# Graph attention layer of a four-layer network: odd units with exponentials taken straight from the sum, and the maximum with one on VectorE

## The reference

```
h = jnp.maximum(_layernorm(x, axis=-1), 0.0)
...
x = h @ weight
el = x @ a_l
er = x @ a_r
mask = adj != 0
scores = el[:, None] + er[None, :]
attn = jnp.exp(jax.nn.leaky_relu(scores, negative_slope=0.2))
attn = jnp.where(mask, attn, 0.0)
denom = jnp.maximum(attn.sum(axis=-1, keepdims=True), 1e-12)
A = attn / denom
out = A @ x + b
```

## Time and profile before

| | us |
|---|---|
| median of 3 runs | 2030.96 (2030.25 to 2031.25) |
| the profiled execution | 2032.97 |
| its span in the trace | 2031.2 |
| attention layer, first y to last y | 597.2 to 868.0 |

### The profile page before, as it was taken

One profiled execution on the slowest core, in us unless ns is written; L12 is line 12 of the kernel. 1 busy time (PEld: TensorE's weight loads), 2 busy tenths in 40 slices (PEclk: granted clock), 3 DMA queues, 4 the chain that ended last, 5 costly groups with the idle time before them and its releaser, 6 DMA issues.

```text
span 2031.2 us, 24901 instructions
## 1 busy us (share of the span) xinstructions
PE 1867.2 (92%) x9423; PEld 1309.6 (64%) x9423; DVE 1505.4 (74%) x2278; ACT 1366.1 (67%) x1760; POOL 13.4 (1%) x15
## 2 busy tenths in 40 slices
PE   4877889699988999999999989899999999999998
PEld 4877888488878989955555556544555555554554
DVE  6222226888877888887878753499898898988986
ACT  4222221466668999988777630399898898988984
POOL 0000000000010000000000000000000000000000
PEclk9999999899999999989999999999999999999999
DMA  9999997688866767669999789533343333334230
GB/s 382 424 424 424 424 425 279 238 323 314 318 250 221 270 243 265 249 219 361 354 327 363 265 311 373 178 119 114 114 154 116 114 119 117 132 123 146 99 99 21
DMA packets 88794, 498.12 MB, mean 245 GB/s; under 512 B 9265, under 2 KB 13362, under 8 KB 39266
## 3 DMA queue, kind: packets, MB, share of 16 engines
q1 hardware_dynamic: 84354, 494.34, 65.1%
q10 hardware_dynamic: 4320, 2.20, 0.4%
HBM read 456.55 MB, written 39.94 MB: 244 GB/s over the span
## 4 chain that ended last, share of the span: by engine, by line
PE 52%; DMA 15%; ACT 14%; DVE 14%; issue 5%; SPq 0%; ACTq 0%; DVEq 0%
PE bank L1972 15%; DMA work<-in_adj_rows 12%; PE bank L1946 4%; ACT work L755 4%; PE bank L1785 3%; ACT work L750 3%; PE bank L1787 3%; PE bank L1786 3%; PE bank L1858 2%; DVE work L1581 2%; PE bank L1980 2%; PE bank L1981 2%; ACT work L906 2%; PE bank L1979 2%; PE bank L1863 2%
## 5 line engine op out<-in xcount | busy, mean ns | idle before, releaser
L1972 PE MATMUL bank<-work,reg 128*128 128x512 f32 x760 | 359.2, 597 | 14.6 <-DVE ring L1532 7.9
L906 ACT ACTIVATE work<-x,e 128x512 f32<-128x512 f32 x552 | 355.1, 709 | 0.4 <-ACT linebuf L871 0.4
L1581 DVE TENSOR_TENSOR work<-work,ring 128x1536 f32<-128x1536 f32 x184 | 321.2, 1749 | 9.2 <-ACT work L906 9.0
L1696 PE MATMUL bank<-reg,ring 128*128 128x128 f32 x2048 | 251.0, 284 | 52.3 <-DMA ring<-in_adj_units 29.7
L1696 PEld LDWEIGHTS bank<-reg,ring 128*128 128x128 f32 x2048 | 243.4, 199 | 58.8 <-issue 37.7
L1816 PE MATMUL bank<-reg,ring 128*128 128x129 f32 x2048 | 242.8, 281 | 26.0 <-DVE ring L1275 25.7
L1816 PEld LDWEIGHTS bank<-reg,ring 128*128 128x128 f32 x2048 | 238.2, 197 | 29.9 <-DVE ring L1275 19.1
L1972 PEld LDWEIGHTS bank<-work,reg 128*128 128x128 f32 x760 | 142.6, 190 | 136.2 <-issue 112.0
L1979 PE MATMUL bank<-s_lo,h_hi 128*128 128x512 f32 x240 | 186.0, 775 | 4.9 <-DVE a_lo L1560 3.7
L1275 DVE SCALAR_TENSOR_TENSOR ring<-ring,work 128x2048 f32<-128x2048 f32 x64 | 147.2, 2300 | 39.3 <-ACT work L755 39.2
L1170 DVE TENSOR_TENSOR a_lo<-ring,a_hi 128x2048 fp32r<-128x2048 f32 x64 | 147.5, 2315 | 17.9 <-ACT a_hi L706 17.5
(11 more groups left out here) (295 smaller groups left out, 3073.7 us busy)
## 6 DMA issues: line engine op xcount, KB each, us to landing
ring<-in_adj_units SPq DMA_DIRECT2D x320, 1024.0 KB, 5.5
work<-in_adj_rows SPq DMA_DIRECT2D x38, 1024.0 KB, 22.6
ring<-masks SPq DMA_DIRECT2D x64, 512.0 KB, 5.7
ring<-in_adj_rows SPq DMA_DIRECT2D x26, 1024.0 KB, 22.4
masks<-work SPq DMA_DIRECT2D x48, 512.0 KB, 8.7
masks<-ring SPq DMA_DIRECT2D x16, 512.0 KB, 8.2
x<-lines SPq DMA_DIRECT2D x8, 768.0 KB, 10.4
ring<-lines SPq DMA_DIRECT2D x8, 768.0 KB, 7.9
```

What stands on the lines that cost most here:

```text
L906: last = act.activation(tiles(n)[:, k * W:(k + 1) * W], guard(c, k), ACT.Sigmoid, bias=e6[:, t * SCORES + k:t * SCORES + k + 1], scale=-1.0)
L1581: dve.tensor_tensor(tv, tv, spread(ring[:, ring_at("out", g, q * W, W)], HEADS, 1), ALU.mult).then_inc(s_y, 1)
L1696: last = pe.matmul(o, ring[:, first:first + P], reg1[:, t * P:(t + 1) * P], start=t == 0 and i == 0, stop=t == T - 1 and i == Q - 1)
L1972: return pe.matmul(bank[1 + k][:, :], reg1[:, t * P:(t + 1) * P], tiles(c * T + t)[:, k * W:(k + 1) * W], start=t == 0, stop=t == T - 1)
```

## The change

Every second unit (n odd, `straight(n)`) is made in another way. ACT takes all its four quarters as Exp straight from `reg4` with the bias `er08`, with no rectifier, and there is no exponential of the whole unit and no quarter on DVE. DVE then takes the maximum with 1 over the whole unit in place (128 x 2048), counts it on a new semaphore `s_gone`, waits for it, and does y(n). Even units stay as they were. The counts of `s_gmax` and `s_grelu` now go by even units.

```
-        def by_dve(n):
-
-            return 2 if n % 2 else 1
+        def straight(n):
+
+            return n % 2 == 1
...
+        s_gone = sem("gat_at_least_one")
...
-                    for q in range(by_dve(n), Q):
+                    for q in range(0 if straight(n) else 1, Q):
                         m = g * Q + q
-                        last = act.activation(gunit(n)[:, q * W:(q + 1) * W], reg4[:, at(c, W, 0, W)], ACT.Relu,
-                                              bias=er08[:, m:m + 1])
-                    last.then_inc(s_grelu, 1)
-                    act.wait_ge(s_gmax, n + 1)
-                    act.wait_ge(s_grelu, n + 1)
-                    act.activation(gunit(n), gunit(n), ACT.Exp).then_inc(s_gexp, 1)
+                        last = act.activation(gunit(n)[:, q * W:(q + 1) * W], reg4[:, at(c, W, 0, W)],
+                                              ACT.Exp if straight(n) else ACT.Relu, bias=er08[:, m:m + 1])
+                    if straight(n):
+                        last.then_inc(s_gexp, 1)
+                    else:
+                        last.then_inc(s_grelu, 1)
+                        act.wait_ge(s_gmax, n // 2 + 1)
+                        act.wait_ge(s_grelu, n // 2 + 1)
+                        act.activation(gunit(n), gunit(n), ACT.Exp).then_inc(s_gexp, 1)
...
-                for q in range(by_dve(n)):
-                    m = g * Q + q
-                    last = dve.tensor_scalar(gunit(n)[:, q * W:(q + 1) * W], reg4[:, at(c, W, 0, W)],
-                                             er08[:, m:m + 1], 0.0, ALU.add, ALU.max)
-                last.then_inc(s_gmax, 1)
+                dve.tensor_scalar(gunit(n)[:, 0:W], reg4[:, at(c, W, 0, W)], er08[:, g * Q:g * Q + 1], 0.0,
+                                  ALU.add, ALU.max).then_inc(s_gmax, 1)
...
-                    if n + 1 < C * G:
+                    if n + 1 < C * G and not straight(n + 1):
                         gat_max(n + 1)
...
                     dve.wait_ge(s_gexp, n + 1)
+                    if straight(n):
+                        dve.tensor_scalar(gunit(n), gunit(n), 1.0, None, ALU.max).then_inc(s_gone, 1)
+                        dve.wait_ge(s_gone, n // 2 + 1)
                     y = ring[:, ring_at("gat", g)]
                     dve.scalar_tensor_tensor(y, y, 0.0, gunit(n), ALU.not_equal, ALU.mult).then_inc(s_gy, 1)
```

## The result

The changed kernel takes 2029.57 us (median of 20 runs, 2027.31 to 2032.22), the kernel before 2031.7 us (20 runs, 2028.32 to 2037.65). The medians are 2.1 us apart. The ratio over all runs is 0.9985, 95% interval 0.9979 to 0.9991 (the quotient of the medians alone is 0.9989): faster by 0.15%, 3 us, and less than the 0.2% that the prediction set as the bound for faster. The profiled execution took 2029.65 us, with a span of 2027.9 (forecast 2029.9; before 2032.97, with 2031.2).

A forecast was written before the change was run, and what follows sets the result against it. One chain bounds each chunk: DVE's node results, a quarter, ACT's exponential and `root`, unit 5, ACT's remaining units. Terms -1.1 - 1.8 - 0.35 + 0.15 = -3.1 us take the median from 2030.96 to 2027.9; range 2021.5 to 2034.5.

The forecast's parts named there:

- wide maximum: DVE's in-place maximum over 2048 numbers in each odd unit, taken at 1.22 us, plus 0.03 for its semaphore wait.
- node results start: On DVE, node results start 2.21 us after y(1) instead of 3.00, as the quarters for unit 3 are gone.
- first quarter of unit 5: ACT starts unit 5's four quarters at 14.54 us, 5.33 after the exponential of unit 4 starts.
- y(5): On DVE, y(5) at 18.44 us instead of 18.75; of 0.79 us won, 0.48 have gone.
- first chunk, change at y(9): First chunk, order set by the layer before: -1.1 us, between -0.4 and -2.
- second chunk: Chunk without `gat_project` and `store_hT`: y(9) at 31.13 us against 32.94 measured before, -1.8 us.
- third to seventh chunk together: Five steady chunks, each 33.35 us instead of 33.42: -0.35 us.
- last chunk to its last y: Last chunk, which ends with y(7): +0.15 us.
- the walk: One attention-layer chunk retraced from y(1) with measured distances: 33.35 us instead of 33.42, DVE setting the pace after y(5).
- Rival 1: DVE's maximum costs more, up to 2.29 us each, 3.2 us per chunk more, total up to 2052 us; chance 0.12.
- Rival 2: DVE's 2.0 us wait for unit 5 vanishes, seven chunks each gain 2.0, total 2014 us; chance 0.07.
- Rival 3: PE becomes the bound through low-clock spells, 34.1 us per chunk with two in each, total about 2033 us; chance 0.09.

The follow-up runs named there:

- `root` early: Changed kernel with root (logarithm and exponential of the norm) moved on ACT between unit 4's quarters and its exponential; 2015.15 us, ratio to before 0.9916.
- units 1, 3, 5 and `root` early: Changed kernel with unit 7 made as before and root moved on ACT between unit 4's quarters and its exponential; 2013.76 us, ratio to before 0.9902.

## Why the prediction was right

The mechanism held, and so did its times. From the start of the node results to the next y(1) they count from y(1) at 0 in the chunk from 702.64:

| step | forecast | measured |
|---|---|---|
| wide maximum | 1.22 | 1.220 (median of 32) |
| node results start | 2.21 | 2.21 |
| y(2) | 6.48 | 6.49 |
| ACT starts exponential of unit 4 | 9.21 | 9.21 |
| first quarter of unit 5 | 14.54 | 14.54 |
| y(5) | 18.44 | 18.46 |
| y(6) | 21.68 | 21.69 |
| y(7) | 27.28 | 27.28 |
| next y(1) | 33.35 | 33.34 |
| first chunk, change at y(9) | -1.1 | -0.9 |
| second chunk | -1.8 | -1.7 |
| third to seventh chunk together | -0.35 | -0.4 |
| last chunk to its last y | +0.15 | +0.15 |

- The sum of -3.1 us came out as -2.9 at the last y (865.73 to 862.82); the span fell by 3.3, of which 0.4 us arose behind the layer. That the total agrees this well is in part luck. The 0.02 us of the walk hold for the steady chunks, but the layer's first y alone lies anywhere from 595.5 to 597.7 us in the seven profiles with unit 1 straight, and single runs of the kernel before spread over 9 us.
- One reading was loose: "three engines within 10% of the period" is true of ACT and PE, while DVE, at 29.09 of 33.42 us, is 13% below. Nothing in the walk uses it.
- The seven quarters from 717.18 (four Exp, three Relu) end after 4.38 us: six distances of 0.61 and one duration of 0.71, the same as for Relu alone. Exp costs ACT the same as Relu at this size.
- The weighed price of the maximum went to the row: 1.22 us, not the 1.13 us estimated from the cycles in "VectorE: DVE Perf Modes" of the Trainium skill.
- In the first chunk the maximum of unit 5 took 2.06 us beside POOL, as the quarter in the earlier trace rows had let one fear; it is one of 32.
- Rival 1 (a dear maximum) did not come, but its slope did: 3.79 us per chunk for 1.25 us on each of the four, three of them in the chain. Rival 2 (DVE's wait goes) did not come by itself, and came with `root` early: 2.05 us per chunk, against 2.0 in the rival. Rival 3 (PE's clock falls more often) did not come; the clock fell less often, see below.

One thing was less good: that one reordering would bring what the change did not was in the text only as the condition of rival 2, called out of reach because of the order, though the order is a line of the kernel.

## What to carry to other kernels

When an instruction is taken from a busy engine, look first at which of its instances stands ahead of the chain's hand-over: here one of four carried the gain (0.79 us per chunk), and the others gave nearly all of it back with what they added behind it (unit 7 0.46 us, units 1 and 5 together 0.25). Where three engines are within some 13% of the period, walk one period with the measured distances before and after; counting ACT's work said that 3.1 us per chunk were to be had, the walk said 0.07, and the chunks gave 0.1. And where an engine waits in front of work on which a slow, independent step (here two table loads) follows, move that step into the wait.

## What was not expected

- PE's clock. Before, PE waited 1.6 to 2.5 us for y(2) in seven chunks, and behind three of these waits (2.51, 2.16 and 2.15 us) the granted clock was 0.50, as at 748.38; behind another of 2.16 it was 1.00. With the change the same wait is 0.4 to 1.2 us, and in no chunk behind the first did the clock fall:

```profile
711.48 11.27 PE L1820 MATMUL bank<-reg,ring 128*128 128x129 f32 x96 [1.12 <-DVE ring L1279]
...
732.26 10.99 PE L1820 MATMUL bank<-reg,ring 128*128 128x129 f32 x96 [1.41 <-DVE ring L1279]
```

  The rival had asked whether more waits might lower the clock: two waits of 1.1 to 1.4 us in a chunk left it at 2.4 GHz, and next to waits of 2.15 or 2.16 us before it was at 1.2 GHz in two cases of three. With the maximum taken twice PE waits 2.66 to 2.67 us once in each of the third to seventh chunks, and the granted clock is 0.50 next to each of the five. By "TensorE: Matmul & The Clock Gate" of the Trainium skill, Part 1, low is the clock's state at rest and work releases it; the trace agrees in so far as the clock stayed up where the waits were short. The low spells cost nothing before either: the chunks with them are as long as those without, 33.4 us.
- Behind the layer the clock is at 0.50 for a while in every kernel: for 13.7 us before, 6.8 with the change, and with `root` early from 859 to 869 us, next to a wait of PE of 3.88 us, and 3.4 us more later. In that profile the span fell by 11.5 us where the last y had come 13.5 earlier. It would be wrong to read this as gains that the next layer takes back: the time from the last y to the end of the span lies between 1164.4 and 1170.1 us in the twelve profiles, with no order by when the layer ended (before 1165.4, with `root` early 1167.0, with units 1, 3, 5 and `root` early 1165.6), and the ratio over all five runs gives 14 us.
- With unit 5 alone straight, two kinds of chunk alternate, 33.2 and 33.5 us. The rows above show where they part. ACT starts the quarters of unit 5 at 15.32 in both, and they end 2.55 us later; the maximum starts 0.10 us behind them in the one kind (as in the walk) and 0.45 in the other. The semaphore event of ACT and the landed load of the unit are there in time in both, and the granted clock is 1.00 in both. In the layer of all twelve profiles only two more waits of DVE, of those over 0.15 us, end more than 0.15 us behind what they waited for. What holds DVE for these 0.35 us in every second chunk, no run shows; a mean over chunks would hide it.
